# Graph attention over gathered edges: one software pipeline, or two loops with a table of value rows between them

## The chip, the cores and the metric

The kernel runs on one core of a Trainium2 chip. The metric is device time in microseconds: before the change the median of three runs is 2274.02 us (2271.47 to 2278.88). The engines are TensorE (PE, with its weight loads PEld), VectorE (DVE), ScalarE (ACT), GpSimd (POOL) and SyncE (SP), which issues most DMAs.

## The reference

The model has four parts in a row on 1250 nodes of 512 features, each on the layer-normed input and added to it. Only the first and the sums of the third are touched:

```
q, k, v = (x @ W + b).reshape(n, 4, 512)                # 4 heads
alpha = einsum(q[dst], k[src]) / sqrt(512)              # one score for each edge and head
attn  = softmax of alpha over the edges of one dst
agg   = segment_sum(attn * v[src], dst)
x_attn = agg + x @ Wskip + bskip
h = x_attn @ Wlin + blin + x_attn[:, :512]; layer norm  # first part
agg   = segment_sum(edge_attr, dst) / count             # third part
```

There are 21250 edges, sorted by dst (17 for a node on average, with its loop). The second part is a mixture of low-rank experts, the fourth self-attention with a mixture of experts.

## The kernel before

Products run in float32r in three passes (`three_pass`, L130): each operand is split into a high part (ScalarE, a copy that rounds) and a low part (VectorE, source minus high part).

**What is prepared.** Wq and Wk are multiplied into one matrix for each head, Wv, Wlin and the residual into another (`vl`). So a score is (normed x of dst, times the matrix: the projection `t`) times the normed x of src, and the values are gathered rows of x, weighted and summed first and multiplied by `vl` afterwards. `graph_attention` (L764) makes the projections in 80 units of 12 products (head, chunk of 250 nodes, 128 rows); ScalarE adds the bias, writes `t_out` (L1089) and issues the store to `t_store`.

**The edge loop.** The nodes are 50 windows of 25; a window's edges are a stretch of the sorted list, read as 500 slots (125 partitions by 4). Five windows are a tile of 125 nodes; there are ten tiles. For window t:
- POOL gathers 500 rows of 2 KB from `xn_store` with four indirect DMAs (`gather`, L1005) into one of four buffers, once the value product of window t-4 is done. It waits for the landing of one gather (`landed`) before it issues the next one. It also subtracts the high part from half of the rows (L1030), turns the dst numbers into offsets (L1017 to L1019) and makes the mask (L1024).
- TensorE turns the rows in four steps (`turn_rows`, L1387), ScalarE and VectorE split each step (L1106, L1225), and TensorE makes the scores of 100 (4 heads by 25 nodes) by 500 (L133 to L135), one step of window t with the turning of one step of window t+1. A product with a 0/1 mask puts -1e30 on the edges of other windows (L1394).
- VectorE takes the maximum (L1238), joins it to a running table (L1239) and makes the bias `nb` (L1240). ScalarE takes the exponential and its sum (L1132). TensorE turns the probabilities (L1427); split again (L1141, L1265), they weight the rows (`values`) into 100x512. ScalarE scales these by the reciprocal sum (`y_rows`, L1148), TensorE turns them (L1435), and ScalarE and VectorE split them into the tile's `yt_hi`, `yt_lo`.
- Edge attributes are loaded for each window, split (L1128, L1276) and summed by a one-hot matrix (L1246, `edge_sums`, L1407).
- One window after each tile's last, TensorE multiplies the tile's 500 turned rows by `vl` (`outputs`: 48 products, then `add_out`, L1291); a pair of tiles is normalised in three steps later (`finish`).

The order on each engine is the order of the calls written out in its block: nothing is planned at run time. SP's queue holds in each turn the index load, the attribute load, parts of `t_raw` every few windows, a 513 KB write of blank rows that the last stage needs (`blanks`, L925, 41 of them), and every tenth window loads and stores of the tiles. Ahead of its first turn stand five loads of `acc` (L938). The loop is in a hardware loop over passes, for windows with over 500 edges; with these inputs it runs once.

Then comes `dense_stages` (L1502), the second and third part, whose edge-free units TensorE bounds, and `self_attention`.

## Time and profile before

| | |
|---|---|
| device time, median of 3 runs | 2274.02 us |
| the profiled execution's own time | 2281.38 us |
| its span | 2279.3 us |
| granted TensorE clock, mean | 0.909 |
| busy: PE, DVE, ACT, POOL | 82%, 59%, 40%, 34% |
| projections, 250 to 374 us | PE busy 119.9 us, clock 0.97 |
| edge loop, 374 to 1257 us | PE 642.0, DVE 557.4, ACT 366.8, POOL 442.1 of 883 us; clock 0.86; DMA 0.38 |
| dense stages and self-attention, 1275 to 2279 us | PE 890.8 of 1004 us; clock 0.94; DMA 0.22 |

The profile follows one execution. Busy time counts instructions that compute; the granted clock is TensorE's, as a share of 2.4 GHz, averaged over two levels (1.2 and 2.4 GHz). Idle time is put down to what ended it. A matmul row's duration is about 0.16 us longer than the distance to the next one, since products are pipelined: steps are read from start to start.

### The profile page before, as it was taken

What the parts mean: (1) busy time and instruction counts of PE and PEld (TensorE: products, weight loads), DVE (VectorE), ACT (ScalarE), POOL (GpSimd) and SP (SyncE); (2) the same over time, 40 slices, a digit from 0 to 9 for tenths busy, and PEclk for the clock granted to TensorE, in tenths of its full rate; (3) what the DMA queues carried; (4) which work ended last, traced back from release to release, by engine and by line L of the source; (5) the groups of instructions that cost most, each with busy time, mean ns of one, the idle gap of its engine ahead of it and who ended that gap; (6) DMA issues with size and microseconds to landing.
All of it is one profiled execution on the core that took longest, in us unless ns stands there. A gap on an engine that the chain in (4) does not pass through costs nothing. (4 is left out here: it accounts for less than half of the span.)

```text
span 2279.3 us, 32000 instructions
## 1 busy us (share of the span) xinstructions
PE 1859.0 (82%) x10998; PEld 1562.7 (69%) x10998; DVE 1349.0 (59%) x3024; ACT 906.4 (40%) x1712; POOL 771.1 (34%) x777
## 2 busy tenths in 40 slices
PE   8997798586776776766877589999999989889686
PEld 6765697365655555555656469989878888778575
DVE  6252112556567566666775535556557868768766
ACT  4331244344434334434434212333335555555521
POOL 0000013456445445545643001111314444444244
PEclk9999898798898888988978799999998999999889
DMA  6843345344443433343421230201420111120442
GB/s 223 254 132 111 137 135 140 119 128 125 123 120 104 118 113 111 118 120 96 106 71 49 88 97 1 83 29 37 150 70 22 33 41 27 28 55 9 166 144 98
DMA packets 178678, 224.10 MB, mean 98 GB/s; under 512 B 88753, under 2 KB 119984, under 8 KB 177010
## 3 DMA queue, kind: packets, MB, share of 16 engines
q1 hardware_dynamic: 112633, 140.69, 20.2%
q0 software_dynamic: 49760, 62.92, 9.7%
q10 hardware_dynamic: 16136, 18.64, 2.3%
q8 instruction: 76, 1.25, 0.2%
q14 instruction: 73, 0.59, 0.1%
HBM read 177.87 MB, written 65.38 MB: 107 GB/s over the span
## 5 line engine op out<-in xcount | busy, mean ns | idle before, releaser
L1005 POOL DMA_INDIRECT edge_rows<-xn_store,edge_index x200 | 259.8, 1299 | 378.5 <-issue 138.6
L1387 PE MATMUL psum<-ident,edge_rows 125*128 125x125 f32 x800 | 149.3, 320 | 145.7 <-DVE edge_xt_lo L1225 84.8
L2472 POOL TENSOR_TENSOR mprob<-mprob,mrden 125x1250 f32<-125x1250 f32 x80 | 181.6, 2271 | 245.5 <-DVE mrden L2578 245.4
L1387 PEld LDWEIGHTS psum<-ident,edge_rows 125*128 125x128 f32 x800 | 115.6, 168 | 184.5 <-DVE edge_xt_lo L1225 96.1
L1106 ACT ACTIVATE edge_xt_hi<-psum 128x500 fp32r<-128x500 f32 x200 | 116.3, 588 | 242.7 <-PE psum L1387 242.5
L1225 DVE TENSOR_TENSOR edge_xt_lo<-psum,edge_xt_hi 128x500 fp32r<-128x500 f32 x200 | 132.8, 674 | 120.2 <-ACT edge_xt_hi L1106 118.7
L2501 ACT ACTIVATE mprob<-psum,mbias 125x1250 f32<-125x1250 f32 x80 | 104.3, 1304 | 172.3 <-DVE mbias L2587 172.3
L2585 DVE TENSOR_REDUCE mmin<-psum 125x1 f32<-125x512 f32 (+1 forms) x240 | 127.1, 584 | 49.4 <-PE psum L2744 48.8
L2762 PE MATMUL psum<-ident,mprob 125*125 125x125 f32 x800 | 120.6, 297 | 33.0 <-DVE ptm_lo L2592 26.2
L2762 PEld LDWEIGHTS psum<-ident,mprob 125*125 125x125 f32 x800 | 103.1, 196 | 49.9 <-DVE ptm_lo L2592 35.8
L1030 POOL TENSOR_TENSOR edge_rows_lo<-edge_rows,edge_rows_hi 125x512 fp32r<-125x512 f32 x100 | 126.7, 1295 | 24.5 <-ACT edge_rows_hi L1122 23.5
L2592 DVE TENSOR_TENSOR ptm_lo<-psum,ptm_hi 125x500 fp32r<-125x500 f32 (+1 forms) x240 | 126.3, 582 | 2.0 <-ACT ptm_hi L2507 2.0
L2744 PE MATMUL psum<-k_stack,q_chunk 128*125 128x512 f32 (+1 forms) x480 | 116.7, 381 | 2.9 <-PEq L123 2.9
L133 PE MATMUL psum<-ptm_hi,v_hi 125*128 125x250 f32 x400 | 115.1, 288 | 4.4 <-DVE ctx_lo L2598 4.4
L2507 ACT ACTIVATE ptm_hi<-psum 125x500 fp32r<-125x500 f32 (+1 forms) x240 | 110.1, 516 | 16.2 <-PE psum L2762 15.1
L134 PE MATMUL psum<-ptm_lo,v_hi 125*128 125x250 f32 x400 | 113.4, 283 | 0.0
L135 PE MATMUL psum<-ptm_hi,v_lo 125*128 125x250 f32 x400 | 112.6, 282 | 0.0
L133 PE MATMUL psum<-xt_hi,fc_hi 128*128 128x250 f32 x320 | 96.1, 300 | 17.7 <-DVE hid_lo L2006 14.5
L133 PE MATMUL psum<-edge_xt_hi,t_hi 128*100 128x500 f32 x200 | 108.4, 542 | 1.2 <-DVE t_lo L1232 1.2
L1122 ACT ACTIVATE edge_rows_hi<-edge_rows 125x1024 fp32r<-125x1024 f32 x100 | 105.8, 1060 | 0.0
L2744 PEld LDWEIGHTS psum<-k_stack,q_chunk 128*125 128x125 f32 x480 | 88.1, 197 | 19.9 <-issue 3.6
L133 PE MATMUL psum<-xt_hi,qk_hi 128*128 128x250 f32 x320 | 91.0, 284 | 3.7 <-ACT t_out L1089 3.7
(527 smaller groups left out, 5585.5 us busy)
## 6 DMA issues: line engine op xcount, KB each, us to landing
slots_in<-blank_rows SPq DMA_DIRECT2D x40, 513.0 KB
t_store<-t_out ACTq DMA_DIRECT2D x80, 125.0 KB, 1.8
q_chunk<-q_store SPq DMA_DIRECT2D x40, 250.0 KB, 5.4
edge_attr<-in_attr SPq DMA_DIRECT2D x50, 125.0 KB
t_raw<-t_store SPq DMA_DIRECT2D x10, 600.0 KB, 9.6
moe_xg<-slots_in SPq DMA_DIRECT2D x17, 256.5 KB, 3.7
raw_WvT<-in_WvT SPq DMA_DIRECT2D x4, 1024.0 KB, 7.0
raw_WskipT<-in_WskipT SPq DMA_DIRECT2D x4, 1024.0 KB, 7.4
```

What stands on the lines that cost most here:

```text
L133: nc.tensor.matmul(out, lh, rh, start=start, stop=False)
L134: nc.tensor.matmul(out, lh, rl, start=False, stop=False)
L1005: nc.gpsimd.indirect_dma_start(xe[t % 4][:, s, :], None, g.xn_store, bass.IndirectOffsetOnAxis(ap=index[t % 4][:, s, 0:1], axis=0)).then_i ...
L1030: last = nc.gpsimd.tensor_tensor(xe_lo[t % 4][:, s, :], xe[t % 4][:, s, :], f32(xe_hi[t % 2][:, s, :]), ALU.subtract)
L1106: nc.scalar.activation(xt_hi[:, k, :], x_bank(KT * t + k), ACT.Copy).then_inc(x_top, 1)
L1225: nc.vector.tensor_tensor(xt_lo[:, k, :], x_bank(KT * t + k), f32(xt_hi[:, k, :]), ALU.subtract).then_inc(x_low, 1)
L1387: last = nc.tensor.transpose(x_bank(n)[:, s * P:(s + 1) * P], xe[t % 4][:, s, k * 128:(k + 1) * 128], g.ident[0:P, 0:P])
L2472: nc.gpsimd.tensor_tensor(prob[:, n % 4, :], prob[:, n % 4, :], rden[:, n % 4:n % 4 + 1].broadcast_to([P, N]), ALU.mult).then_inc(p_ready, 1)
L2585: last = nc.vector.tensor_reduce(low[:, s, q:q + 1], score[:, a:b], AX.X, ALU.min)
L2592: nc.vector.tensor_tensor(pt_part(n, 1, j0, j1), piece(q), f32(pt_part(n, 0, j0, j1)), ALU.subtract).then_inc(tp_free, 1)
L2744: last = nc.tensor.matmul(score[:, a:b], qs[:, half, n // 2, cols], g.k_stack[:, n // 2, a:b], start=half == 0, stop=half == 1)
L2762: last = nc.tensor.transpose(piece(q)[:, j - j0, :], prob[:, n % 4, j * P:(j + 1) * P], g.ident[0:P, 0:P])
```

## The change

The edge loop is cut in two, and work moves between engines:

- **Projections.** VectorE now makes the low part straight from PSUM beside ScalarE's high part, in three banks; `t_store` holds both, window by window, and SP stores a part of 1 MB for every 4 units. In the loop one load of 400 KB and one copy on ScalarE (800 columns) replace load, copy and subtraction.
- **Loop one (50 windows)** gathers into five buffers, makes scores, probabilities and value rows and writes each window's scaled rows (200 KB) to `y_store`. POOL issues gather t+4, and only then waits for the landing of gather t+3; its subtractions are VectorE's (`rows_lo` in two halves). VectorE makes the mask in one operation from the indices. A fixed bound takes the place of the table of maxima: `nb` is one operation behind the maximum.
- **Loop two (40 turns: 10 tiles by 4 heads)** loads a tile's rows by head from `y_store` (`y_load`, 5 DMAs), turns them (125 columns at a time instead of 100), splits them, makes the outputs, with two banks for the output and two for the turned rows, and makes the edge sums, for which indices and attributes are loaded again. POOL clears one-hot columns there. The loads of `acc` and of the first expert weight (1 MB) stand between the two loops in SP's queue, ahead of the attribute load of window 2.
- **Blank rows** are written during the dense stages.

```
             for h in range(HEADS):
+                for c in range(NC):
+                    i = NC * h + c
+                    for m in range(KT):
+                        u = KT * i + m
+                        dve.wait_ge(u_top, u + 1)
+                        nc.vector.scalar_tensor_tensor(part[i % 2][:, :, 1, m, :], unit_bank(u).rearrange("p (w n) -> p w n", n=WIN),
+                                                       g.tcols[:, KT * h + m:KT * h + m + 1], f32(part[i % 2][:, :, 0, m, :]),
+                                                       ALU.add, ALU.subtract).then_inc(u_low, 1)
+                        if c == 2 and 1 <= h < HEADS - 1:
+                            m_low_of(h + 1, m)
+                        if c == 3:
+                            low_of(v_lo[h], v_raw[h], v_hi[h], m, v_top, KT * h + m + 1, v_low)
...
             def gather(t):
-                pool.wait_ge(index_in[t % 4], 16 * (t // 4) + 16)
-                if t >= 4:
-                    pool.wait_ge(y_done, t - 3)
+                pool.wait_ge(index_in[t % RING], 16 * (t // RING) + 16)
+                if t >= RING:
+                    pool.wait_ge(y_done, t - RING + 1)
                 for s in range(SLOTS_E):
-                    nc.gpsimd.indirect_dma_start(xe[t % 4][:, s, :], None, g.xn_store,
-                                                 bass.IndirectOffsetOnAxis(ap=index[t % 4][:, s, 0:1], axis=0)
-                                                 ).then_inc(xe_in[t % 4], 16)
+                    nc.gpsimd.indirect_dma_start(xe[t % RING][:, s, :], None, g.xn_store,
+                                                 bass.IndirectOffsetOnAxis(ap=index[t % RING][:, s, 0:1], axis=0)
+                                                 ).then_inc(xe_in[t % RING], 16)
             def landed(t, turn):
-                used = len(range(t % 4, WINDOWS, 4))
-                pool.wait_ge(xe_in[t % 4], turn * (16 * SLOTS_E * used) + 16 * SLOTS_E * (t // 4 + 1))
+                used = len(range(t % RING, WINDOWS, RING))
+                pool.wait_ge(xe_in[t % RING], turn * (16 * SLOTS_E * used) + 16 * SLOTS_E * (t // RING + 1))
                 pool.sem_inc(xe_ready, 1)
...
-            def rest(t):
-                pool.wait_ge(xe_top, 2 * t + 2)
-                pool.wait_ge(x_done, KT * t + KT)
-                for s in (2, 3):
-                    last = nc.gpsimd.tensor_tensor(xe_lo[t % 4][:, s, :], xe[t % 4][:, s, :], f32(xe_hi[t % 2][:, s, :]),
-                                                   ALU.subtract)
-                last.then_inc(xe_pool, 1)
...
-                offsets(0)
-                others(0)
-                for t in range(1, 3):
+                skip_over(pool)
+                gather(1)
+                landed(0, turn)
+                parts_over(pool)
+                for t in range(2, RING):
                     gather(t)
                     landed(t - 1, turn)
+                for t in range(1, WINDOWS):
+                    if t + RING - 1 < WINDOWS:
+                        gather(t + RING - 1)
+                    if t + RING - 2 < WINDOWS:
+                        landed(t + RING - 2, turn)
...
-                    rest(t)
-                    if t + 1 < WINDOWS:
-                        offsets(t + 1)
-                        others(t + 1)
-                    if t + 2 < WINDOWS:
-                        landed(t + 2, turn)
-                    if t + 3 < WINDOWS:
-                        gather(t + 3)
+                    clear(t)
                     c, step = divmod(t, 2 * PER_TILE)
-                    if step == 8 and c < FIN:
...
             def maxima(t):
                 dve.wait_ge(s_done, KT * t + KT)
                 link(nc.vector.tensor_reduce(col(gmax, t), score, AX.X, ALU.max))
-                link(nc.vector.scalar_tensor_tensor(col(tmp, t), col(gmax, t), const(t), col(m_tab, t), ALU.add, ALU.max))
-                nc.vector.tensor_scalar(col(nb, t), col(tmp, t), const(t), -scale, ALU.subtract, ALU.mult).then_inc(m_ready, 1)
-                nc.vector.tensor_scalar(col(top, t), col(tmp, t), -scale, None, ALU.mult).then_inc(m_ready, 1)
+                nc.vector.scalar_tensor_tensor(col(nb, t), col(gmax, t), -scale, col(bound, t), ALU.mult, ALU.min).then_inc(m_ready, 1)
+            def others(t):
+                dve.wait_ge(index_in[t % RING], 16 * (t // RING) + 16)
+                if t:
+                    dve.wait_ge(s_done, KT * (t - 1) + 2)
+                edges, shift = own_edges(t)
+                nc.vector.scalar_tensor_tensor(other[:], edges.unsqueeze(2).broadcast_to([P, SLOTS_E, HW]), shift,
+                                               bc(ids[0:P, :], SLOTS_E), ALU.add, ALU.not_equal).then_inc(other_ready, 1)
...
+            def rows_lo(t, q):
+                if q == 0:
+                    dve.wait_ge(xe_top, 2 * t + 2)
+                    dve.wait_ge(x_done, KT * t + KT)
+                nc.vector.tensor_tensor(xe_lo[t % RING][:, halves(q), :], xe[t % RING][:, halves(q), :], f32(xe_hi[t % 3][:, halves(q), :]),
+                                        ALU.subtract).then_inc(xe_low, 1)
...
+                others(0)
                 for k in range(KT):
                     x_lo(0, k)
+                for t in range(WINDOWS):
+                    more = t + 1 < WINDOWS
                     if more:
                         for k in range(KT - 1):
                             x_lo(t + 1, k)
+                    maxima(t)
                     if more:
                         x_lo(t + 1, KT - 1)
+                        others(t + 1)
+                    rows_lo(t, 0)
+                    sums(t)
+                    rows_lo(t, 1)
+                    p_lo(t)
+                yt_lows(0), yt_lows(1)
+                hots(0)
+                attr_lo(0)
+                for n in range(TURNS):
+                    r, h = divmod(n, HEADS)
+                    if n + 2 < TURNS:
+                        yt_lows(n + 2)
+                    for t in sums_behind(n + 1):
+                        hots(t)
+                        attr_lo(t)
+                    if h == 0 and r:
+                        add_out(r - 1)
+                        edge_sums(r - 1)
                     for c in range(FIN):
+                        finish(c, n - 2 * HEADS * c)
                 add_out(NT - 1)
+                edge_sums(NT - 1)
+                nc.vector.tensor_copy(bound[:], nb[:])
...
+                for t in range(WINDOWS):
+                    for k in range(KT):
+                        scores(t, k)
+                        if k == 0:
+                            mask(t)
+                        if t + 1 < WINDOWS:
+                            turn_rows(t + 1, k)
                     if t:
                         values(t - 1)
+                    turn_prob(t)
+                turn_values(0), turn_values(1)
+                values(WINDOWS - 1)
+                for n in range(TURNS):
+                    outputs(n)
+                    if n + 2 < TURNS:
+                        turn_values(n + 2)
+                    for t in sums_behind(n):
+                        edge_sums(t)
...
+                for t in range(3):
+                    t_load(t)
+                for t in range(WINDOWS):
+                    if t + RING < WINDOWS:
+                        sp.wait_ge(xe_ready, t + 1)
+                        sp.wait_ge(other_ready, t + 1)
+                        edges_in(t + RING)
+                    if t + 3 < WINDOWS:
+                        t_load(t + 3)
+                    if t:
+                        y_store(t - 1)
+                    if t == WINDOWS - 1:
+                        sp.wait_ge(y_done, WINDOWS - RING + 1)
+                        y_load(0)
+                sp.wait_ge(s_done, KT * WINDOWS)
+                sp.wait_ge(other_ready, WINDOWS)
+                sp.wait_ge(xe_ready, WINDOWS)
+                sp.wait_ge(xe_low, 2 * WINDOWS)
+                firsts = [edges_in(t) for t in range(RING)]
+                attr_load(0, firsts[0]), attr_load(1, firsts[1])
+                y_load(1)
+                y_store(WINDOWS - 1)
+                sp.dma_start(fin.beta[:], row_view(w["beta"])).then_inc(xin_in, 16)
+                sp.dma_start(fin.last_xin[:], pair(w["x"], FIN)).then_inc(xin_in, 16)
+                for i in range(2):
+                    sp.wait_ge(y_stored[i], 16 * (WINDOWS // 2))
                 for c in range(NC):
                     sp.dma_start(g.acc[:, 2 * c:2 * c + 2, :], pair(g.base_store, c)).then_inc(base_in, 16)
+                sp.dma_start(g.fc1_raw0[:], w["fc1T"][0].rearrange("(k p) n -> p k n", p=128)).then_inc(g.fc1_in, 16)
                 for t in range(WINDOWS):
+                    if t + RING < WINDOWS:
+                        sp.wait_ge(hot_ready, t + 1)
+                        firsts.append(edges_in(t + RING))
+                    if t + 2 < WINDOWS:
+                        attr_load(t + 2, firsts[t + 2])
...
+            for i in range(BLANKS):
+                sp.wait_ge(u_done, UNITS + KT * (i * (LAST - 1) * NE // BLANKS))
+                blanks(2 * i, 2)
+            blanks(2 * BLANKS, 1)
...
```

## Rows read from the trace of the kernel before

**Rows 1.** Busy time by stage: stretch, length, each engine's busy time.
```profile
250.00:374.00 124.00, 119.92 (x978) 118.33 (x976) 17.52 (x27) 50.24 (x104) 8.11 (x10) 0.97 0.41 128
...
374.00:1257.00 883.00, 642.01 (x3280) 493.17 (x3280) 557.41 (x1200) 366.77 (x703) 442.10 (x497) 0.86 0.38 109
```

**Rows 2.** Line L1132, the exponentials: ns min/median/max, first and last start.
```profile
L1132 ACT ACTIVATE prob<-psum,nb x50: 667/677/681, 388.9 to 1235.6; 100x500 f32<-100x500 f32 x50
```

**Rows 3.** Waits in the edge loop: who for what, us, times, longest.
```profile
POOL edge_rows L1005 <- DMA edge_rows<-xn_store,edge_index: 134.4, 28, 10.0
...
POOL edge_rows L1005 <- PE psum L135: 103.9, 13, 13.7
...
ACT prob L1132 <- DVE nb L1240: 92.2, 40, 5.6
```

**Rows 4.** POOL's timeline in a window: start, us, engine, line, operation.
```profile
603.77 1.27 POOL L1005 DMA_INDIRECT edge_rows<-xn_store,edge_index  x1 [4.86 <-DMA edge_rows<-xn_store,edge_index]
...
608.38 1.21 POOL L1005 DMA_INDIRECT edge_rows<-xn_store,edge_index  x1 [0.30 <-issue]
...
609.61 2.54 POOL L1030 TENSOR_TENSOR edge_rows_lo<-edge_rows,edge_rows_hi 125x512 fp32r<-125x512 f32 x2
```

**Rows 5.** The gathers' line L1005: from issue to landing.
```profile
DMA to landing us min/median/max: 3.9/5.5/17.5
```

**Rows 6.** One line's instructions: L1239, the running maximum.
```profile
L1239 DVE SCALAR_TENSOR_TENSOR max_new<-gmax,const_table,max_table x50: 219/2137/5475, 388.4 to 1234.3; 100x1 f32<-100x1 f32 x50
```

**Rows 7.** VectorE's timeline in the same window.
```profile
609.39 2.78 DVE L1239 SCALAR_TENSOR_TENSOR max_new<-gmax,const_table,max_table 100x1 f32<-100x1 f32 x1
```

**Rows 8.** TensorE's timeline in a window without waits.
```profile
569.90 0.47 PE L133 MATMUL psum<-edge_xt_hi,t_hi 128*100 128x500 f32 x1
...
572.12 0.63 PE L1407 MATMUL psum<-edge_attr_hl,edge_hot 125*125 125x130 f32 x4
...
572.59 0.44 PE L133 MATMUL psum<-vl_hi,yt_hi 128*125 128x512 f32 x1
...
583.76 0.39 PE L133 MATMUL psum<-edge_rows_hi,pt_hi 125*100 125x512 f32 x1
...
586.54 0.58 PE L1427 MATMUL psum<-ident,prob 100*125 100x100 f32 x4
```

**Rows 9.** Groups by line and form: busy us, mean ns, idle before.
```profile
L1225 DVE TENSOR_TENSOR edge_xt_lo<-psum,edge_xt_hi 128x500 fp32r<-128x500 f32 x200 | 132.8, 674 | 120.2 <-ACT edge_xt_hi L1106 118.7
...
L1260 DVE TENSOR_TENSOR edge_rows_lo<-edge_rows,edge_rows_hi 125x1024 fp32r<-125x1024 f32 x50 | 61.3, 1225 | 9.2 <-ACT edge_rows_hi L1122 9.2
...
L1265 DVE TENSOR_TENSOR pt_lo<-psum,pt_hi 125x400 fp32r<-125x400 f32 x50 | 28.5, 570 | 107.4 <-ACT pt_hi L1141 107.4
...
L1106 ACT ACTIVATE edge_xt_hi<-psum 128x500 fp32r<-128x500 f32 x200 | 116.3, 588 | 242.7 <-PE psum L1387 242.5
...
L1122 ACT ACTIVATE edge_rows_hi<-edge_rows 125x1024 fp32r<-125x1024 f32 x100 | 105.8, 1060 | 0.0
...
L1115 ACT ACTIVATE t_hi<-t_raw 128x400 fp32r<-128x400 f32 x50 | 26.8, 536 | 0.0
...
L1089 ACT ACTIVATE t_out<-psum,t_cols 128x250 f32<-128x250 f32 x80 | 37.4, 468 | 111.5 <-PE psum L135 104.0 <-DMA t_store<-t_out 6.6 <-ACT t_out L1089 0.9
```

**Rows 10.** A gather beside VectorE's rows_lo: POOL's and VectorE's timelines.
```profile
426.53 1.93 POOL L1005 DMA_INDIRECT edge_rows<-xn_store,edge_index  x1 [0.31 <-issue]
...
426.15 1.23 DVE L1260 TENSOR_TENSOR edge_rows_lo<-edge_rows,edge_rows_hi 125x1024 fp32r<-125x1024 f32 x1 [0.37 <-ACT edge_rows_hi L1122]
427.29 0.57 DVE L1271 TENSOR_TENSOR yt_lo<-psum,yt_hi 128x400 fp32r<-128x400 f32 x1
```

**Rows 11.** The page's DMA issues: KB each, us to landing.
```profile
t_raw<-t_store SPq DMA_DIRECT2D x10, 600.0 KB, 9.6
```

**Rows 12.** SyncE's timeline: the five loads of acc.
```profile
377.96 16.48 SPq L938 DMA_DIRECT2D acc<-base_store  x5
```

**Rows 13.** VectorE's timeline at the loop's end.
```profile
1257.18 0.69 DVE L1291 TENSOR_TENSOR acc<-acc,psum 125x512 f32<-125x512 f32 x1 [12.18 <-PE psum L135]
```

More of the change, by code:

```diff
@@ L41 @@
 ATTR = 2 * EDGE_D + 2
+RING = 5
+NC_W = WINDOWS // NC
 BANK = 512
@@ L957, in _ @@
+                    if step == 5 and c < FIN:
                         if c:
```

635 lines of the change are left out of this document (295 added, 340 removed).

## The prediction

> **What bounds the kernel now.** I read four views in this order. First the stages (busy time by window) [rows 1]: in the 124 us before the edge loop TensorE is busy 119.9 us at a granted clock of 0.97, so it is the bound there. In the edge loop, 374 to 1257 us, it is busy 642 of 883 us at 0.86, and no other engine is above 642: nobody is full, so the loop is held by waits. The exponentials, one for each of the 50 windows, start at 388.9 and end at 1235.6 [rows 2]: 846.7/49 = 17.3 us a window. Then the waits of that stretch [rows 3]: POOL waits 134.4 us for landings and 103.9 us for TensorE (the gather's buffer is freed by the value product, which every fifth window stands behind 11 us of outputs), and ScalarE waits 92.2 us for the bias `nb`. Then the timelines of one window. POOL waits 4.86 us for the landing of the gather issued before, only then issues the next four DMAs (603.77 to 609.59), and then does 2.54 us of subtractions [rows 4]. A gather lands 5.5 us after its issue in the median, 17.5 at most [rows 5]. So issue (5.8), landing and POOL's own work stand one after the other, and that is the period. VectorE's `max_new`, an operation on 100x1 elements that can take 0.22, took 2.14 in the median [rows 6]; the one at 609.39 took 2.78, to 612.17, just the end of POOL's subtractions at 612.15 [rows 4, 7]: it was held by them, on the path to the exponential. The chain view shows the last stage only and doesn't reach this loop.
>
> **The change, part by part.** All terms are against the profiled execution (span 2279.3, device time 2281.4, 7 above the median of 2274.0); the difference is applied to the median.
>
> *TensorE's work in loop one.* Score steps with transposes take (572.12 - 569.90)/2 = 1.11 us each [rows 8]; four and a mask (the estimate for its four small products is 0.25) are 4.7. A value product is 586.54 - 583.76 = 2.78, turning the probabilities 0.5 (0.58 with its tail). Together 8.0 us a window at the full 2.4 GHz. Outputs, turned values and edge sums leave this loop.
>
> *VectorE in loop one.* Four `x_lo` (0.67 each), one maximum (500 columns too, 0.67), five operations on 100x1 elements at 0.22 [rows 6], `pt_lo` 0.57, and two `rows_lo` of 1.23 instead of one, since POOL's half moves here [rows 9]. The new mask operation has 400 columns; its bounds are 0.22 and 1.23, and I take 0.57, the 400-column `pt_lo`. Sum 8.05 as durations; the operation behind a `rows_lo` started 1.14 after it, not 1.23 [rows 10], so with 0.09 less for each wide one it is 7.3 of occupancy, 7.6 with the hand-overs. *ScalarE:* four `x_hi` 2.35, two `rows_hi` 2.12, exponential 0.68 [rows 2] with an estimated 0.5 of small ones, `y_rows` (512 columns) 0.68 like it, `p_hi` 0.54 by the 400-column row, and the copy of the split projections, now 800 columns (bounds 0.54 for 400 and 1.06 for 1024; I take 0.87): 7.7, or 7.0 of occupancy [rows 9]. VectorE no longer splits the projections, because both parts come from memory.
>
> *The chain between them.* With TensorE starting window t at 0: the last score ends at 4.4, `x_lo` of the third step ends at 5.1, maximum and `nb` at 6.0, exponential and its sum at 6.8; TensorE does the value product of t-1 until 7.4 and then finds the probabilities ready. The projection copy ends at 7.9, exactly when the next scores start at 7.9. So TensorE bounds, with almost no slack for ScalarE and VectorE. 8.0 at a clock of 0.97 [rows 1] is 8.2; I take 8.6 for the hiccups.
>
> *POOL.* It only gathers. Four issues take 5.8 and 0.3 between: 6.05. The landing of gather k is awaited only after k+1 is issued, with five buffers instead of four, so issue and landing overlap. A gather started 0.38 after a `rows_lo` began took 1.93 instead of 1.21 [rows 10]: up to 0.72 more. With 2.5 us of such operations in 8.6, about 30% of the gathers meet one: +0.3 to 0.8 a window, 6.9 in all, still under 8.6. From y_done of a window to the transposes that need the block TensorE has about 9.5 us of work, POOL about 7.5: 2 us of slack.
> The Trainium skill (SBUF — State Buffer, "SBUF: two separate sides") says that VectorE and GpSimd take the shared port as an exclusive lock for a whole instruction, and warns that a VectorE operation can keep GpSimd from writing descriptors. By that rule moving the subtractions to VectorE takes time off `max_new` and puts it on the gathers; the two rows agree with both halves, and if it met all four gathers the loop would be the third rival below.
>
> *Start of loop one.* Before, transposes start at 374 [rows 1]. Now window 0's projections are loaded only when the last 1 MB part is stored. A 600 KB load from that tensor took 9.6 to land [rows 11]; for store and load of 1 MB and 400 KB the bounds are 7 and 25, I take 15: scores start at 389.5. Building both parts in the stage before costs a second reader of each bank on VectorE, 0.45 beside ScalarE's 0.47 in units of at most 1.5 (80 within the 124 us of rows 1), where ScalarE idled 111.5 us in all, nearly all for TensorE [rows 9]; with three banks it hides. Its own DMA issues leave ScalarE; the bytes double, DMA was at 0.41 there [rows 1]. If that cover went, 0.5 x 80 = 40 us.
>
> *Loop two.* 40 turns, each 12 products ((583.76 - 572.59)/4 = 2.79) and four transposes (0.4: the step of 1.11 less three products of 2.78/12 = 0.23): 127.6. Fifty edge sums of 0.47 (572.12 to 572.59) 23.5 [rows 8]. Sum 151, at 0.97 156 us. Before it, the last `p_lo`, the last values and the wait for the first y_load: 9. VectorE's share of a turn (a split of 0.67, one or two one-hot and attribute operations of 0.3 to 0.4, the sums) is 2 to 3 of 3.7 us and hides; the finishing of a pair of tiles (four operations of 512 columns near 0.7 and chains of small ones, in three steps) overruns its turns by about 0.7 a step: 12 x 0.7 = 8.
>
> *A new stall.* SP issues the five loads of `acc` before the loop, and that took it 16.48 us [rows 12], because the queue is full. Now they and a 1 MB weight load stand in front of attribute load 2, on which edge sum 2 on TensorE and `attr_hi(2)` on ScalarE (with the next `yt_hi` behind it) wait. TensorE gets there some 11 us after its first output; the data are there about 30 us after. 20 us once; bounds 5 (the queue drains at once) and 35.
>
> *Blanks.* 41 writes of 513 KB leave the loop's DMA queue, where they collide with gathers' last rows, and go to the dense stage, where TensorE bounds and DMA is little used. +4 (0 to 12).
>
> *Tail.* The last twelve us of outputs before the add at 1257.2 [rows 13] become 2.8; that is in the sum. +2 for the last edge sums.
>
> *Sum.* 389.5 + 50 x 8.6 + 9 + 156 + 20 + 8 + 2 = 1014.5 against 1257.2: -242.7. With blanks -238.7. 2274.0 - 239 = 2035 us.
>
> **Rivals.**
> (B) *The handshakes on VectorE bound loop one.* Two full `rows_lo` stand ahead of `p_lo` and the next `x_lo`; VectorE is at 7.6 of 8.2. For: every score step already hangs on a hand-over ScalarE to VectorE to TensorE. Against: the walk above closes at 8. If each window loses 1.3 more: T = 9.9, +65: 2100.
> (C) *The gathers bound it.* If `rows_lo`, mask and sums meet all four: 4 x (1.51 + 0.72) = 8.9, and with the wait for the freed buffer not overlapped 10.5: +95, 2130. For: the stretched gather [rows 10]; against: a gather that starts before such an operation kept its 1.21, so a meeting needs a start inside it.
> (D) *Slower: landings.* If the gathers' landings, not the order on POOL, set the period (loads of 400 KB and stores of 200 KB a window now share the engines), loop one stays at 17.3 and loop two comes on top: +50 x 8.7 = 435, 2470. It decides from a period of (1257.2 - 389.5 - 199)/50 = 13.4 us (199: all terms behind loop one and the blanks); at that the kernel is even. For: landings of up to 17.5 [rows 5]. Against: the median is 5.5, under the 6.05 of the next issue, and the 513 KB writes beside them leave.
> (E) *The change does not do what it says in loop two:* turned values are a round trip through memory, and if the rows come late, TensorE pauses and is granted the low level (1.2 GHz): 156 becomes 311, 2190.
> (F) *Everything overlaps:* T = 8.1 and a first stall of 8: 2035 - 25 - 12 = 1998.
>
> **Chances.** Forecast 0.56, B 0.20, C 0.12, D 0.03, E 0.04, F 0.05. The range reaches from F, 1998, past B to 2115 and leaves out most of C, D and E, about 0.18. 0.3% is about what a measurement of this kernel can tell from no change. Slower by more only D: 0.03; within 0.3% 0.01; faster 0.96.
>
> **What would show it.** Exponentials 8 to 9.3 us apart; `nb` ready without an operation of over 0.3 us ahead of it; POOL with a wait for TensorE (a freed buffer), not for landings; granted clock about 0.95 in loop one; loop two near 190 us with one pause of about 20 us in its first tile, ended by `edge_attr`. Wrong it is if TensorE's transposes wait for POOL in most windows (C, D), if its idle time is ended by `edge_xt_lo` (B), or if the dense stage is longer by over 12 us.

## The result: 2.7% slower, where 10% faster was predicted

| | before | after | predicted |
|---|---|---|---|
| time, us | 2276.45 (2271.47 to 2287.39, 4 runs) | 2339.12 (2337.82 to 2341.79, 4 runs) | 2035 (1998 to 2115) |
| ratio to before | | 1.027 [1.023, 1.031] | |
| span of the profiled run, us | 2279.3 | 2340.0 | |

Times below are medians of the runs in the fast state; one run of e6, of 2790.92 us at a granted clock of 0.615, is left out (with it e6's median is 2342.17).

The edge work did become shorter: its last addition, at 1257.18 before [rows 13], starts at 1043.83, 213 us earlier. All that stands behind it, the dense stages and the self-attention, became 274 us longer and took all of it. The stages of the kernel after, in the columns of [rows 1] (stretch, length, busy time of TensorE, its weight loads, VectorE, ScalarE and GpSimd, granted clock, DMA share, GB/s):

```profile
374.00:775.00 401.00, 394.65 (x2388) 312.73 (x2388) 353.65 (x698) 334.90 (x597) 270.62 (x193) 0.98 0.81 200
775.00:1040.00 265.00, 179.58 (x842) 145.21 (x843) 116.91 (x324) 42.33 (x93) 21.11 (x57) 0.84 0.29 98
1040.00:1240.00 200.00, 160.28 (x1126) 143.51 (x1125) 103.65 (x275) 51.15 (x121) 19.80 (x11) 0.90 0.23 77
1240.00:1450.00 210.00, 11.98 (x102) 11.73 (x100) 7.06 (x25) 2.39 (x7) 4.75 (x2) 0.53 0.13 55
1450.00:1560.00 110.00, 13.32 (x92) 13.07 (x92) 9.25 (x18) 7.62 (x17) 0.00 (x0) 0.54 0.20 75
```

The first line is loop one: TensorE is busy 98% of it, where the old loop had 73%. The second is loop two, with 85 us of idle TensorE. The fourth and fifth are the loss: in 320 us of the dense stage TensorE works 25, and the DMA engines, which ought then to be the bound, are at a share of 0.13 and move 55 GB/s. The waits say who is late (engine, line, releaser: us, times, longest), the issues of the blank rows and SyncE's timeline say why:

```profile
ACT w_hi L1821 <- DMA w_raw<-in_W: 302.6, 2, 294.9
...
ACT edge_attr_hl L1191 <- DMA edge_attr<-in_attr: 134.7, 36, 31.1
...
PE psum L1492 <- DVE edge_attr_hl L1316: 76.5, 20, 29.0
...
ACT prob L1159 <- DVE nb L1273: 22.3, 50, 1.5
...
PE psum L1469 <- DMA y_tile<-y_store: 11.7, 1, 11.7
```

```profile
L1690 SPq DMA_DIRECT2D slots_in<-blank_rows x41: 592/9650/11259, 1141.4 to 1436.5; - x41
```

```profile
1141.39 306.39 SPq L1690 DMA_DIRECT2D slots_in<-blank_rows  x41
1447.83 1.56 SPq L1717 DMA_DIRECT2D w_raw<-in_W  x1
1449.44 41.95 SPq L1719 DMA_DIRECT2D w_raw<-in_W  x1
```

The landing of the load of L1717, after its issue:

```profile
DMA to landing us min/median/max: 96.7/96.7/96.7
```

SyncE issues the 41 blank transfers one after the other. The first twelve take about 0.6 us each, and from the fourteenth on an issue stands 9.6 to 11.3 us with few exceptions; I read this as a full queue, in which the next transfer finds room only when one has drained. A transfer has 525,312 bytes (the 513 KB of the page), and 525,312 bytes in 9.65 us are 54 GB/s. The weight load behind them is due at about 1240 (e15 issues it at 1239.28, e16 at 1240.87) and is issued at 1447.83, 207 us late. It then lands 96.7 us after its issue, where e1's takes 5.0. So some 207 us of the pause come from SyncE standing and some 92 from the landing. Before, the same transfers were issued once in each 17.3 us window, and half of those issues took 0.65 us or less, though the longest stood 13.03.

Loop one's exponentials and gathers, to be set against [rows 2] and [rows 3] (min/median/max ns and starts; busy, mean ns, idle before):

```profile
L1159 ACT ACTIVATE prob<-psum,nb x50: 677/678/680, 388.7 to 772.7; 100x500 f32<-100x500 f32 x50
```

```profile
L1053 POOL DMA_INDIRECT edge_rows<-xn_store,edge_index x200 | 280.5, 1403 | 243.3 <-issue 181.6 <-PE psum L137 52.3 <-DMA edge_rows<-xn_store,edge_index 9.4
```

The period (from one window's exponential to the next one's) is (772.7 - 388.7)/49 = 7.84 us, was 17.3; GpSimd's waits for landings fell from 134.4 to 9.4 us, and ScalarE's for `nb` from 92.2 to 22.3.

### The profile page after: what moved, and what is told of

Its sections match the earlier page's. It is cut to its first block and busy times, and to the rows that moved or that the text cites. A ratio compares the mean times of both kernels' runs of the same rounds, so it can differ in the third digit from the quotient of the medians.

```text
span 2340.0 us, 31896 instructions
## 1 busy us (share of the span) xinstructions
PE 1781.9 (76%) x10958; PEld 1518.8 (65%) x10958; DVE 1303.4 (56%) x2945; ACT 920.2 (39%) x1702; POOL 622.8 (27%) x526
## 5 line engine op out<-in xcount | busy, mean ns | idle before, releaser
L1053 POOL DMA_INDIRECT edge_rows<-xn_store,edge_index x200 | 280.5, 1403 | 243.3 <-issue 181.6
L135 PEld LDWEIGHTS psum<-xt_hi,fc_hi 128*128 128x128 f32 x320 | 62.1, 194 | 315.3 <-DVE hid_lo L2060 311.3
L2033 DVE TENSOR_TENSOR w_lo<-w_raw,w_hi 128x512 fp32r<-128x512 f32 x16 | 10.7, 684 | 302.9 <-ACT w_hi L1821 302.5
L1428 PE MATMUL psum<-ident,edge_rows 125*128 125x125 f32 x800 | 120.6, 274 | 23.1 <-POOLq L1060 23.1
L1767 POOL TENSOR_TENSOR x_res<-x_res,xs_chunk 125x1024 f32<-125x1024 f32 x5 | 12.3, 2453 | 466.5 <-DVE xs_chunk L2007 466.5
L1821 ACT ACTIVATE w_hi<-w_raw 128x512 fp32r<-128x512 f32 x16 | 9.7, 627 | 302.6 <-DMA w_raw<-in_W 302.6
L1428 PEld LDWEIGHTS psum<-ident,edge_rows 125*128 125x128 f32 x800 | 97.2, 143 | 45.2 <-POOLq L1060 23.5
L1294 DVE TENSOR_TENSOR edge_rows_lo<-edge_rows,edge_rows_hi 125x1024 fp32r<-125x1024 f32 x100 | 121.2, 1212 | 0.0
```

Source lines behind the costliest of these rows:

```text
L135: nc.tensor.matmul(out, lh, rh, start=start, stop=False)
L1053: nc.gpsimd.indirect_dma_start(xe[t % RING][:, s, :], None, g.xn_store, bass.IndirectOffsetOnAxis(ap=index[t % RING][:, s, 0:1], axis=0)). ...
L1294: nc.vector.tensor_tensor(xe_lo[t % RING][:, halves(q), :], xe[t % RING][:, halves(q), :], f32(xe_hi[t % 3][:, halves(q), :]), ALU.subtrac ...
L1428: last = nc.tensor.transpose(x_bank(n)[:, s * P:(s + 1) * P], xe[t % RING][:, s, k * 128:(k + 1) * 128], g.ident[0:P, 0:P])
```

## Experiments on the blanks

All ratios are to the kernel before, with 95% intervals.

**e1: sixteen blocks in one transfer**, at the same place.

```
-            for i in range(BLANKS):
-                sp.wait_ge(u_done, UNITS + KT * (i * (LAST - 1) * NE // BLANKS))
-                blanks(2 * i, 2)
+            for i in range(BLANKS // 8):
+                sp.wait_ge(u_done, ...)
+                blanks(16 * i, 16)
```

> The changed kernel, its blank rows still written in the dense stages from the same place in SyncE's queue, but as 5 transfers of 16 blocks and one of 1, instead of 40 of 2 and one of 1. Same bytes (21 MB), same packets of 43,776 bytes. Theory (pair): a transfer of 2 blocks is served by two DMA engines, 6 packets of 1.61 us each, so 41 of them take some 400 us and the expert weights stand behind them; 16 blocks are served by 16 engines, all bytes are out in about 50 us, and the 294 us pause of TensorE goes: 2339 - 275 = 2065 us (2050 to 2090). Rival (bytes): writing 21 MB to memory beside the dense work is what takes long; time stays within 20 us of 2339.

Measured 2041.23 us (2037.59 to 2042.67), 0.895 [0.894, 0.897]: 298 us under the change as it was, and 9 below the theory's range, which counted on 275. The same bytes now land in 16 us for each 4.1 MB transfer, and TensorE is busy again where the hole was:

```profile
L1690 SPq DMA_DIRECT2D slots_in<-blank_rows x6: 549/558/1414, 1134.3 to 1206.0; - x6
...
DMA to landing us min/median/max: 15.0/16.1/23.3
```

```profile
1050.00:1250.00 200.00, 173.89 (x1259) 157.84 (x1259) 108.98 (x275) 54.77 (x133) 24.36 (x12) 0.93 0.51 171
1250.00:2036.00 786.00, 705.72 (x4618) 626.44 (x4616) 559.68 (x1361) 360.00 (x684) 286.38 (x227) 0.96 0.23 68
```

**e2: the same 41 transfers, rows outermost.** `"(i p) d -> p i d"` in place of `"(i p) d -> i p d"` on both sides.

> The changed kernel, each blank transfer written row by row (128 rows outermost, 2052 bytes each), still 41 transfers at the old places. Theory (pair): rows spread over 16 engines, a transfer takes about 2 us instead of 9.65, the pause goes: 2065 us, as with 16 blocks, within 15 us of it. Rival (bytes): 2339. Rival (small packets): 10,500 packets of 2 KB slow the weight loads, 2100 to 2150.

Measured 2064.63 us (2062.84 to 2068.05), 0.906 [0.904, 0.907]. This is as the theory said. e1 kept the packets and changed the count, e2 kept the count and changed the packets (2052 bytes); the bytes are the same in both, and nearly all of the loss is gone in both. So it is the outermost dimension that cost it. The 23 us between e1 and e2 are not explained here. Two blocks outermost were carried at 54 GB/s; a transfer of sixteen (4.1 MB) landed in 16.1 us, and here all 41 were issued in 110 us, about 190 GB/s. The Trainium skill (DMA: Bandwidth & Descriptors, "Why a DMA increments its semaphore by 16 and not by 1") says that a transfer is spread over the largest number of engines up to 16 that divides the outermost size of both sides: two here. The trace agrees (a DMA share of 0.13, two engines of 16, in the stretch that the blanks fill), and so does e15 below.

**e3: the kernel before with only the blanks moved**, in their old shape, to the place in the dense stage.

> The kernel before, with one part of the change alone: the 41 blank transfers go from the edge loop to the dense stages, in the same shape. Theory (pair): the dense stage gets the pause of about 275 us here too, and the edge loop gains what the blanks cost its gathers (waits for landings 134 us in all, at most half of it): 2276 + 275 - 40 = 2510 us (2480 to 2550). Rival: the pause comes from something else of the change (the new loops, or what they leave in the queues): 2276 or less.

Measured 2503.93 us (2499.74 to 2507.5), 1.097 [1.095, 1.099], as the theory said: moving one group of transfers costs 225 us (before was at 2279.4 beside it) without anything else of the change. The stretch from the weight load ahead of the blanks to the first store of `x_store` takes 172.3 us before and 468.5 in e3, 173.2 in e1 and 469.9 in the kernel after: the narrow blanks cost 296 to 297 us there in either kernel. The old edge loop gains 65 of them back by being rid of the blanks (its exponentials span 781.5 us for 846.7).

**e15 and e16: is it SyncE that stands, or the loads behind?** Fourteen narrow transfers, about as many as the queue took without standing, and the other 53 blocks in one.

```
-            for i in range(BLANKS):
+            for i in range(14):
...
-            blanks(2 * BLANKS, 1)
+            blanks(28, 2 * BLANKS - 27)
```

> Changed kernel (2339.12 us), with the blanks as 14 transfers of two blocks at the places of the first 14 of 41, and one transfer of the other 53 blocks behind them. The narrow ones still take 9.65 us each on two engines, 135 us in all. Theory (the loss comes through SyncE, which stands once some 14 transfers are under way and sends the weights' loads 210 us late): with 14 it never stands for long, 2041 to 2060 us. Rival (every load whose packets stand behind the blanks on the two engines lands late, even when issued in time): the first weight load lands up to 100 us late, 2090 to 2160 us.

Measured 2599.73 us (2599.18 to 2601.34), 1.141 [1.137, 1.145]: far outside both. The 53 blocks were my mistake, and tell more than the plan. DMA over the stage, and SyncE:

```profile
1400.00:1600.00 200.00, 0.00 (x0) 0.00 (x0) 0.00 (x0) 0.00 (x0) 0.00 (x0) 0.50 0.06 27
```

```profile
1138.75 51.27 SPq L1690 DMA_DIRECT2D slots_in<-blank_rows  x15
1239.28 451.13 SPq L1717 DMA_DIRECT2D w_raw<-in_W  x1
```

53 is prime, and the transfer goes at 27 GB/s with a DMA share of 0.06, one engine of 16: half of the 54 that two blocks get. The issue of the next load stood 451 us, and the load landed 112 us after that (563.5 in all). e16 sends the 53 blocks with rows outermost:

> As the run with 14 transfers of two blocks and one of 53 (2599.73 us), but the one of 53 blocks has its 128 rows outermost, so that all 16 engines share it; the 14 narrow ones stay as they were. Theory (the loss comes through SyncE, which stands while more than some 14 transfers are under way): 2041 to 2065 us. Rival (loads whose packets stand behind the narrow transfers on two engines land up to 100 us late even when issued in time, and so does the wide one): 2090 to 2160 us.

Measured 2193.93 us (2187.45 to 2194.79), 0.964 [0.962, 0.966]: outside the theory, above the rival.

```profile
1138.91 39.73 SPq L1690 DMA_DIRECT2D slots_in<-blank_rows  x14
1178.68 11.23 SPq L1717 DMA_DIRECT2D slots_in<-blank_rows  x1
1240.87 142.79 SPq L1719 DMA_DIRECT2D w_raw<-in_W  x1
```

The weight load was due at 1240.87. Its issue took 142.79 us, and it landed 11.9 us after that (154.7 in all). So in e16 nearly all of the time goes in SyncE standing at the issue, though only 15 transfers lie ahead. The reading that fits is that a wide issue stands as long as one engine's queue is full, here with the rest of the narrow and the wide blanks; no run shows how much falls to each. The rival was right in part: in the kernel after (96.7 us) and in e15 (112) the load also lands about 100 us late once it is issued.

## Experiments on loop one

**e8: the kernel before, blanks at their old place with rows outermost.**

> Kernel before, its 41 transfers of blanks at their old place but with the 128 rows outermost, so that all 16 DMA engines share each. Theory (the two clogged engines held the gathers' rows back: GpSimd waits 134.4 us for landings in it): landings shorten and the loop gains 50 to 130 us, 2150 to 2230 us. Rival (landings are not what sets the old loop's period, another chain takes over at once, as when only the order of the gathers was changed): 2260 to 2285 us.

Measured 2209.58 us (2202.74 to 2218.1), 0.967 [0.964, 0.971]. The theory held: GpSimd's waits for the landing of a gather fall from the 134.4 us of [rows 3] to 32.8, and the period from 17.3 to 16.0. Narrow blanks were already a cost in the old loop.

```profile
POOL edge_rows L1005 <- PE psum L135: 107.0, 16, 14.1
...
POOL edge_rows L1005 <- DMA edge_rows<-xn_store,edge_index: 32.8, 15, 4.6
```

**e12: e8, and VectorE makes all four slots' lower halves** (GpSimd's `rest(t)` is gone, `rows_lo` has a second operation on slots 2 and 3).

> Kernel before with blanks spread over 16 engines (2209.58 us, period 16.0 us), and VectorE makes all four slots' lower halves, so GpSimd has no arithmetic of 512 columns left. Theory (GpSimd's two subtractions, 2.6 us of each group, delay its landings and gathers and hold VectorE's operations at the shared port): period 14.0 to 15.2 us, 2110 to 2170 us. Rival (VectorE's chain from score to values sets the period, and it grows by one operation of 1.2 us): period 16.5 to 17.3 us, 2235 to 2275 us.

Measured 2156.61 us (2154.39 to 2162.06), 0.947 [0.944, 0.951]; period 15.3, just above the theory's 15.2. VectorE gets 1.2 us more of work in each window, and the kernel is faster. The running maximum, 2137 ns in the median in [rows 6], is no longer held:

```profile
L1238 DVE SCALAR_TENSOR_TENSOR max_new<-gmax,const_table,max_table x50: 219/220/2852, 385.7 to 1134.8; 100x1 f32<-100x1 f32 x50
```

But this doesn't show that the hold was the cost. In e4 below the same operation falls to 221 ns in the median, and nothing is gained. e12 takes away the hold and GpSimd's 2.5 us of work together, and doesn't tell them apart. It also gains in two places: the exponentials of all windows span 749.1 us for e8's 784.9 (36 us), and the self-attention, which neither edit touches, takes 616.5 us from the store of `q_store` to the end where e8 takes 637.0. The kernel before (637.6), e3 and e4 have that longer stage too, the kernel after (614.9) and e1 (614.5) the shorter one. In the long ones VectorE stands there in six pauses for which the profile shows nothing that it waited for (the kernel before):

```profile
DVE mbias L2587 <- issue: 11.4, 3, 4.5
DVE mrden L2578 <- issue: 7.4, 3, 2.5
```

Why they come and go is open. About 20 of e12's 53 us are this and not the edge loop.

**e10 and e6: the same on the side of the new kernel**, e1 with GpSimd's half given back. In e6 `rest(t)` stands behind the gathers of t+4, in e10 ahead of them.

```
+                    rest(t)                  # e10: here; e6: behind landed()
                     if t + RING - 1 < WINDOWS:
                         gather(t + RING - 1)
                     if t + RING - 2 < WINDOWS:
                         landed(t + RING - 2, turn)
...
                    rows_lo(t, 0)
                    sums(t)
-                    rows_lo(t, 1)
```

> Changed kernel with 16-block blanks (2041.23 us), and GpSimd makes the lower half of slots 2 and 3 again (two subtractions of 125x512 for each group) in place of VectorE. Theory (the bound moves to GpSimd): four gathers of 1.21 us, 0.9 us of issue between them, two subtractions of 1.30 us and the stretching of gathers and VectorE's operations beside them make a period of 8.4 to 9.4 us where TensorE's work allows 7.85: 2070 to 2120 us, with loop one's gathers above 1.3 us. Rival (TensorE is the bound and has cover for it, VectorE even gains 1.2 us for each group): 2035 to 2047 us, period 7.85.

Measured 2340.21 us (2335.94 to 2344.12), 1.026 [1.022, 1.031]: neither. The period is 13.72 us. GpSimd's subtractions stand behind gathers that wait for the value product, which itself waits for the subtractions (TensorE 197.2 us, GpSimd 262.5):

```profile
POOL edge_rows L1054 <- PE psum L137: 262.5, 45, 6.6
...
PE psum L135 <- POOL edge_rows_lo L1067: 197.2, 46, 4.4
```

> As the run in which GpSimd makes the lower half of slots 2 and 3 (2342.17 us, period 13.72 us), but with these subtractions ahead of group t+4's gathers on GpSimd and not behind them. Theory (that run's period was a closed ring: values of t-1, then the gathers that need its buffer, then the subtractions, then values of t; GpSimd's own work is 4 x 1.21 + 0.9 + 2 x 1.30 = 8.3 us): period 8.4 to 9.4 us, 2065 to 2120 us. Rival (the subtractions and gathers disturb VectorE through the port that the two share, and the walk of VectorE is what grew): period stays above 11 us, over 2200 us.

Measured 2154.83 us (2153.1 to 2155.85), 0.946 [0.943, 0.949]. The order alone gives 185 us, so the ring was real, though the hold on `nb` told below fell with it (3268 ns in the median in e6, 1346 here). The time lies between theory and rival: the period is (878.5 - 387.5)/49 = 10.02, above the theory's 9.4, and `nb`, 159 ns in e1, is a large part of the reason. VectorE's, GpSimd's and ScalarE's timelines:

```profile
611.50 2.83 DVE L1284 SCALAR_TENSOR_TENSOR nb<-gmax,max_bound 100x1 f32<-100x1 f32 x1
...
611.79 2.52 POOL L1067 TENSOR_TENSOR edge_rows_lo<-edge_rows,edge_rows_hi 125x512 fp32r<-125x512 f32 x2
...
614.37 0.68 ACT L1170 ACTIVATE prob<-psum,nb 100x500 f32<-100x500 f32 x1 [3.16 <-DVE nb L1284]
```

An operation on 100 numbers ends at 614.33, just with GpSimd's second subtraction at 614.31, and the exponential waits 3.16 us for it. "GpSimd only gathers" is worth 113 us here (2154.83 - 2041.23), 2.2 us a window. GpSimd's own 8.3 us could explain 0.5 of it; the hold on VectorE's shortest operation, 1346 ns in the median, is by its size most of the rest (ScalarE's wait for `nb` goes from 22.3 us in e1 to 103.1). No run separates the two.

**e4: in the kernel before, gathers issued before the landing of the last ones is waited for.**

```
+                    if t + 3 < WINDOWS:
+                        gather(t + 3)
                    if t + 2 < WINDOWS:
                        landed(t + 2, turn)
-                    if t + 3 < WINDOWS:
-                        gather(t + 3)
```

> The kernel before, with one line order changed on POOL: gather t+3 is issued before the landing of gather t+2 is awaited, with four buffers as before. Theory (serial): issue and landing stand one after the other in the old loop, so the 134 us of waits for landings mostly go, -60 to -130: about 2180 us. Rival (buffers): the next gather then waits for TensorE's value product instead, since four buffers leave no more room; -0 to -20: about 2265.

Measured 2281.97 us (2269.56 to 2289.7), 1.001 [0.999, 1.003]: the rival. The gathers' landing waits are gone from GpSimd's list and come back mostly as waits for TensorE: for the buffer (103.9 before), and for the one-hot block that GpSimd clears next (44.3 before):

```profile
POOL edge_rows L1005 <- PE psum L135: 142.8, 29, 14.0
...
POOL edge_hot L1017 <- PE psum L1407: 115.0, 29, 6.2
```

The hold on the running maximum is gone as well, and ScalarE's wait for `nb` falls from 92.2 to 53.2 us, and still the exponentials span 856.5 us for 846.7. In the old loop neither the order nor that hold bounds by itself.

```profile
L1239 DVE SCALAR_TENSOR_TENSOR max_new<-gmax,const_table,max_table x50: 219/221/4261, 388.7 to 1244.4; 100x1 f32<-100x1 f32 x50
```

**e13: the reverse in the new kernel** (e1, landing first, then gathers, with its five buffers).

> Changed kernel with 16-block blanks (2041.23 us, period 7.85 us, five buffers); the one edit is that GpSimd waits for group t+3's landing before it issues group t+4's gathers. Theory (a landing waited for behind its own issue closes a ring of 4 x 1.21 + 0.9 of issue and 5.3 us of landing, however many buffers there are): period 10.8 to 11.1 us, as with four buffers in that order, 2185 to 2200 us. Rival (the fifth buffer makes up for it, since the gathers start a group earlier): 2041 to 2060 us.

Measured 2185.68 us (2179.1 to 2186.53), 0.958 [0.954, 0.962]. The period, (913.2 - 386.7)/49 = 10.74, is just under the theory's 10.8 and far from the rival; here the order alone is worth 144 us, and every window has its landing wait:

```profile
POOL edge_rows L1053 <- DMA edge_rows<-xn_store,edge_index: 243.2, 46, 6.3
```

**e7 and e11: e1 with four buffers of edge rows**, in the new order and in the old one (`RING = 4`, the four buffers placed so that loop two's tiles don't wait for the last windows).

> Changed kernel with 16-block blanks (2041.23 us), with four buffers of edge rows, as the kernel before has, in place of five; everything else, the order on GpSimd too, is kept. Theory (the order and the short chain free the buffers early enough: a gather has two periods, 15.7 us, for 5.7 us of issue and its landing): within 8 us of 2041. Rival (the fifth buffer is what took GpSimd's 134 us of landing waits and 104 us of buffer waits away): period 8.5 to 9.5 us, 2070 to 2125 us.

Measured 2139.31 us (2136.26 to 2146.06), 0.939 [0.935, 0.942], period 9.84: the theory is out, and the time is a little above the rival's. GpSimd's waits for the value product double, from 94.0 us in e1:

```profile
POOL edge_rows L1053 <- PE psum L137: 198.4, 46, 8.7
```

> As the run with four buffers (2139.31 us, period 9.84 us), but GpSimd waits for group t+2's landing and announces it before it issues group t+3's gathers, as the kernel before does. Theory (with four buffers the gathers of t+3 wait for values of t-1, and the landing of t+2, long there, is announced 5.7 us behind them; the buffer itself isn't missing): 2041 to 2060 us. Rival (the fifth buffer is needed as such): 2120 to 2150 us, or more, since the landing is now waited out too.

Measured 2188.16 us (2186.33 to 2190.57), 0.961 [0.958, 0.964], period 10.83: the rival's "or more", and within 3 us of e13. So with the serial order the fifth buffer is worth nothing, with the new order it is worth 98 us, and the new order is worth 49 us with four buffers and 144 with five. Each is of full use only with the other.

## Experiments on loop two

The predicted pause is there: TensorE stands 29.04 us at the third edge sum, because attribute load 2 is issued behind the base rows and fc1, the first expert weight. TensorE's and SyncE's timelines of the kernel after:

```profile
831.66 1.10 PE L1492 MATMUL psum<-edge_attr_hl,edge_hot 125*125 125x130 f32 x4 [29.04 <-DVE edge_attr_hl L1316]
```

```profile
799.31 13.66 SPq L1000 DMA_DIRECT2D acc<-base_store  x5
813.01 3.71 SPq L1001 DMA_DIRECT2D fc_raw<-in_fc1T  x1
817.66 1.60 SPq L936 DMA_DIRECT2D edge_index<-in_edges  x1
819.44 0.70 SPq L962 DMA_DIRECT2D edge_attr<-in_attr  x1
```

**e5: base rows loaded pair by pair inside loop two** (from e1; `acc_load(t // 10)` where `t % 10 == 1`, fc1 at group 43, `dve.wait_ge(base_in, 16 * (r // 2) + 16)`).

> Changed kernel with 16-block blanks (2041.23 us), and the five loads of the base rows taken from ahead of loop two into it: pair c is issued at group 10c+1, the sum of a tile waits for its own pair alone, fc1's first load goes at group 43. Theory: the pause of 28.96 us at the third edge sum of loop two is attribute load 2 standing behind 2.5 MB of base rows and 1 MB of fc1 on SyncE's queue, so nearly all of it goes and the pauses behind the finish steps stay: 2041 - 25 = 2016 us (2008 to 2028). Rival: the 3.5 MB must move anyway and the attribute loads collide with them group by group, so the pause only spreads over loop two: 2033 to 2045 us.

Measured 2031.43 us (2030.62 to 2037.02), 0.891 [0.888, 0.894]: 10 us better, between theory (2028 at most) and rival (2033 at least). The long pause is gone, but TensorE still waits for attributes, in 19 pauses:

```profile
PE psum L1497 <- DVE edge_attr_hl L1321: 57.8, 19, 6.0
```

In e1 the same wait was 75.5 us, 29.0 of them in the long pause, so the other pauses grew by 11, as the rival had it. TensorE's busy time for the same products in loop two (some 840 records) grew as well, by 10 us. The stretches of e1, e5, e9 and e14, in the columns of [rows 1]:

```profile
783.00:1033.00 250.00, 177.05 (x840) 143.02 (x841) 116.00 (x322) 42.18 (x90) 20.71 (x57) 0.85 0.29 99
783.00:1025.00 242.00, 186.72 (x840) 151.36 (x841) 116.70 (x322) 41.72 (x90) 20.87 (x57) 0.85 0.30 102
782.00:1000.00 218.00, 167.54 (x835) 136.60 (x836) 112.73 (x325) 41.32 (x92) 19.61 (x57) 0.89 0.32 113
781.00:985.00 204.00, 167.82 (x838) 136.95 (x839) 108.05 (x320) 43.11 (x92) 20.89 (x57) 0.92 0.34 121
```

**e9: e5 with four attribute buffers**, filled four groups ahead.

> The version with late base rows (2031.43 us), with four buffers of attribute rows in loop two in place of two, each filled four groups ahead. Theory (what is left of loop two's waits, 57.8 us in 19 pauses of TensorE, is an attribute load issued only two groups ahead on SyncE's shared queue): most of them go, and 35 of the 57.8 us are gained: 1996 us (1985 to 2012). Rival (the pauses come from the order of ScalarE's and VectorE's work around the finish steps, not from the loads): waits only change name, 2022 to 2036 us.

Measured 2004.84 us (2003.63 to 2005.86), 0.880 [0.878, 0.883]: in the theory's range, but not by its sum. The waits for attributes fall by 13 us and not by 35, and those for `y_tile` grow from 11.9 to 19.4; the larger part of the 27 us is TensorE's busy time, which falls by 19 as its granted clock rises from 0.85 to 0.89. Ten pauses are left, and next to them a wait in VectorE for the store of the pair that it is about to overwrite:

```profile
PE psum L1499 <- DVE edge_attr_hl L1323: 44.4, 10, 9.4
...
DVE acc L726 <- DMA base_store<-acc: 34.3, 4, 9.3
```

**e14: e9 with that store a group earlier and the finish steps a head later** (`step == 0` for 1 on SyncE, 11, 12 and 14 for 10, 11 and 13 on VectorE, the node rows' load at 7 for 5).

> The version with four attribute buffers (2004.84 us), where VectorE stands 34.3 us in four waits until a pair of base rows is stored before it overwrites them. The store is issued one group earlier, the three finish steps come one head later, and the load of the node rows two groups later. Theory (TensorE's ten pauses of 44.4 us behind the edge sums are these waits handed on, and a head is worth 4 to 5 us of each of four): 1980 to 1992 us. Rival (the pauses are VectorE's 9 us of finish work between two edge sums, which stays): 2000 to 2008 us.

Measured 1994.36 us (1991.87 to 1997.65), 0.875 [0.872, 0.879]: between theory and rival. VectorE's wait for the store is gone, and TensorE's waits for the attributes fall from 44.4 to 18.1 us; the longest are now those for a load of value rows, 11.9 in one pause in e5 and 19.4 in e9:

```profile
PE psum L1476 <- DMA y_tile<-y_store: 29.7, 5, 11.6
...
PE psum L1499 <- DVE edge_attr_hl L1323: 18.1, 10, 3.7
```

This is the best version run: 12.5% under before, 345 us under the change as it was.

## Why the prediction was wrong

- *Blanks, "+4 (0 to 12)": the step that failed.* They cost 298 us (e1 against the kernel after). I reasoned that they move to a stage where DMA is little used, but the share is a mean over 16 engines, and two of them carry all of it. The step "Blanks" counted bytes and a collision; it didn't ask how long one transfer holds its engines, nor what stands behind 41 of them on SyncE's queue (the weight loads). e1, e2 and e3 show it: in another shape at the same place 2041 and 2065, and alone in the old kernel 2504. The prediction's own sign for it, a dense stage longer by over 12 us, came true.
- *"Where they collide with gathers' last rows": right, and left without a price.* Changing their shape in the old loop (e8) is worth 73 us.
- *Start of loop one:* 389.5 predicted for the first scores; they start at 381.2. The store and load took about 7 us, the lower bound, where I had taken 15.
- *Loop one, 8.6 us a window:* 7.84 from exponential to exponential; from the first scores to the end of the last turning of probabilities (774.9) it takes 394 us for 430, 36 better. The walk's 8.0 was the right sum; the 0.6 of clock and hiccups did not come.
- *POOL.* The claim that issue, landing and own work stand in series and set the old period is not borne out by e4: the order alone does nothing there, because the waits for TensorE take their place. In the new loop it is right (e13). The hold on `max_new` is real (e10 shows it on `nb`), but the claim that it costs the old loop is not: e4 is rid of it for nothing. The half that should fall on the gathers is small and not clear: 1403 ns a gather in the kernel after, 1299 before, and 1218 in e1, whose loop one has the same code and the same period.
- *Loop two and its stall, 9 + 156 + 20 + 8 + 2 = 195:* from 774.9 to the last addition at 1043.8 it is 269. TensorE's work took some 181 rather than 156: the prediction's 151 at a granted clock of 0.84, not 0.97, are 180. The waits are 11.7 + 76.5 = 88 rather than 37. The one stall is 29 (predicted 20, bounds 5 and 35); what I missed are the 47 us in 19 more pauses, two attribute buffers on a shared queue (e9) and VectorE's finish steps with their wait for a store (e14), and the clock that goes with them.
- Together the loop terms give -213 for -243: the start (-8), loop one (-36) and loop two (+74) leave 29. That e1, with blanks at 16 blocks, measures 2041.23 against the forecast's 2035 is luck. Its loops end 220 us earlier, not 243, and the other 23 come from the self-attention, in which the change altered nothing and which the prediction gave no term.
- Of the rivals, B and C didn't come; F's loop one came (7.84 for its 8.1), its short stall didn't. E's pause and low clock came in small: one wait of 11.7 us for the value rows, and 0.84. (By the prediction's own rows E's 311 is 2 x 151 = 302.) D came out on its side, slower, by another mechanism. My 0.03 for "slower" was the chance of that one mechanism only.

## What to carry to other kernels

Ask of every moved DMA what its outermost size is and what stands behind it on its queue, before asking how many bytes it has: a low DMA share can be two engines that are full. A transfer that is harmless once in 17 us is not so 41 times in a row. When buffers and issue order form one ring, changing either alone may show nothing or half, so test them together. And when a total comes out as forecast, compare stage by stage: two misses of 23 us hid each other here.

## What the runs showed of the hardware

- A memory-to-memory transfer with 2 blocks outermost ran at 54 GB/s, with 53 at 27 GB/s; 41 issues of the first kind took SyncE 306 us. A single issue of a weight load behind such transfers took 451 us (e15) and 142.8 us (e16), and the load landed 112 and 11.9 us later.
- A VectorE operation on 100x1 elements with its operands in SBUF was held to 2.83 us by GpSimd's subtraction beside it (e10), though its record begins 0.29 us ahead of it; the 250 operations of 500 columns that read PSUM never took over 0.69 us in that run.
- With its pauses TensorE was granted 0.84 in loop two where loop one had 0.98 (of 2.4 GHz), and 0.53, near its low level, in the stretch in which it waited for weights.
- For the same products of loop two TensorE was busy 186.7 us with 19 pauses for attributes (e5) and 167.5 us with ten (e9).
